# Transfers of the maxima and the spill of the attention rows: issued by ScalarE's queue in place of SP's

## What is computed

```python
qkv = jnp.einsum('bnc,ce->bne', x, w_qkv)          # 16 heads of 8 channels
attn = jnp.einsum('bhnd,bhmd->bhnm', q, k) / scale
attn = jax.nn.softmax(attn, axis=-1)
out = jnp.einsum('bhnm,bhmd->bhnd', attn, v)       # then w_out
...
x = x + _layernorm(_L0_attn_ref(_layernorm(x, axis=-1), ...), axis=-1)
x = x + _layernorm(_L0_ffn_ref(_layernorm(x, axis=-1), ...), axis=-1)
```

## Time and profile before

| | us |
|---|---|
| median of 3 runs | 390.42 (388.07 to 392.32) |
| the profiled execution | 389.27 |
| its span | 387.4 |
| TensorE busy in it | 369.4 (95%) |
| VectorE, ScalarE, GpSimd busy | 305.3, 263.3, 201.9 |

### The profile page before, as it was taken

One profiled execution on the slowest core, in us unless ns is written; L12 is line 12 of the kernel. 1 busy time (PEld: TensorE's weight loads), 2 busy tenths in 40 slices (PEclk: granted clock), 3 DMA queues, 4 the chain that ended last, 5 costly groups with the idle time before them and its releaser, 6 DMA issues.

```text
span 387.4 us, 10179 instructions
## 1 busy us (share of the span) xinstructions
PE 369.4 (95%) x3376; PEld 239.9 (62%) x3376; DVE 305.3 (79%) x775; ACT 263.3 (68%) x498; POOL 201.9 (52%) x521
## 2 busy tenths in 40 slices
PE   7989999998999999999999999999999999998982
PEld 6976655555555757475656565665665656577872
DVE  4238968879999998989998989989999875667540
ACT  2413387787887787868788868787868788753422
POOL 4321041244538384747476646656545648577654
PEclk9998999999999999999999999999999999999997
DMA  1794756385556557554474373747374033223230
GB/s 44 194 208 92 206 131 143 95 200 124 165 120 165 148 138 165 146 136 140 128 181 122 111 185 72 188 128 167 105 185 120 12 105 92 70 62 80 54 85 27
DMA packets 63651, 48.81 MB, mean 126 GB/s; under 512 B 9432, under 2 KB 60504, under 8 KB 63600
## 3 DMA queue, kind: packets, MB, share of 16 engines
q1 hardware_dynamic: 63600, 48.17, 49.0%
HBM read 28.52 MB, written 19.14 MB: 123 GB/s over the span
## 4 chain that ended last, share of the span: by engine, by line
PE 74%; issue 6%; DVE 6%; POOL 5%; SPq 3%; ACT 2%; DMA 2%; POOLq 0%; ACTq 0%; DVEq 0%
PE pvp L475 14%; PE bank_d L573 10%; PE sc L459 9%; PE sc L444 8%; PE bank_d L586 7%; PE bank_d L574 7%; PE bank_d L482 5%; PE bank_a L527 4%; DVE mx L736 3%; PE bank_a L536 2%; PE bank_d L564 2%; POOL rstd L852 2%; PE bank_d L546 2%; DMA den<-pv_dram 1%; PE bank_a L517 1%
## 5 line engine op out<-in xcount | busy, mean ns | idle before, releaser
L736 DVE TENSOR_REDUCE mx<-sc 128x4 f32<-128x1024 f32 x128 | 153.3, 1219 | 23.0 <-PE sc L444 22.3
L608 ACT ACTIVATE pr<-sc 128x1024 f32<-128x1024 f32 x128 | 130.5, 1024 | 19.8 <-PE sc L459 18.9
L475 PE MATMUL pvp<-pr,va 128*32 128x256 f32 x1024 | 68.5, 385 | 0.0
L573 PE MATMUL bank_d<-x3T,wg_sb 128*128 128x256 f32 x160 | 54.7, 424 | 2.4 <-DVE hb L815 2.2
L444 PE MATMUL sc<-ks,qs 48*128 48x256 bf16 x512 | 49.1, 275 | 2.7 <-DVE mx L736 1.7
L459 PE MATMUL sc<-qs,ks 51*128 51x256 bf16 x512 | 49.2, 273 | 0.9 <-ACT pr L608 0.5
L910 POOL TENSOR_TENSOR hw<-hb,rwb 128x256 f32<-128x256 f32 x64 | 45.5, 727 | 4.7 <-DMA rwb<-rw_dram 4.7
L574 PE MATMUL bank_d<-x3T,wu_sb 128*128 128x256 f32 x160 | 47.6, 379 | 0.0
L675 ACT ACTIVATE th<-bank_d 128x256 f32<-128x256 f32 x80 | 30.6, 382 | 21.5 <-PE bank_d L574 20.3
L852 POOL TENSOR_TENSOR rstd<-vareps,mhalf 128x2 f32<-128x2 f32 x64 | 44.5, 695 | 0.0
L482 PE MATMUL bank_d<-ident 128*128 128x128 f32 x264 | 41.2, 301 | 1.5 <-POOL ident L835 1.5
(11 more groups left out here) (80 smaller groups left out, 520.2 us busy)
## 6 DMA issues: line engine op xcount, KB each, us to landing
rwb<-rw_dram SPq DMA_DIRECT2D x32, 256.0 KB, 4.4
qk_dram<-parts SPq DMA_DIRECT2D x32, 192.0 KB, 2.7
qs<-qk_dram SPq DMA_DIRECT2D x32, 192.0 KB, 4.4
ks<-qk_dram SPq DMA_DIRECT2D x32, 192.0 KB, 4.4
qk_dram<-parts SPq DMA_DIRECT2D x32, 128.0 KB, 2.4
pv_dram<-pv_sb SPq DMA_DIRECT2D x16, 256.0 KB, 2.6
x_sb<-in_L_attn_x_dram SPq DMA_DIRECT2D x16, 128.0 KB, 2.6
qk_dram<-parts SPq DMA_DIRECT2D x32, 64.0 KB, 2.0
```

Source lines behind the costliest of these rows:

```text
L475: mm = pe.matmul(pvp[32 * j:32 * j + 32, g, :], values[:, X * c + 4 * g + j, 32 * tt:32 * tt + 32], pr[:, k, c * N:(c + 1) * N], start=(tt ...
L573: pe.matmul(bank_d[bank][:, 0:N], wg_sb[:, ORDER[n], :], x3T[b % 2][:], start=True, stop=True)
L608: nc.scalar.activation(pr[:, 2 * s:2 * s + 2, :].rearrange("p k n -> p (k n)"), sc[PAIR["s2", b, s]][:].rearrange("p u c n -> p (u c n)"), ...
L736: nc.vector.tensor_reduce(mx[b % 2][:, :, :, s].rearrange("p c u -> p u c"), sc[PAIR["s1", b, s]][:], AX.X, ALU.max).then_inc(max_done, 1)
```

## The change

Both blocks of SP's program move to ScalarE's, each right behind the copy whose result it sends. The waits go along: ScalarE now waits for its own copy's semaphore (`max_copied`, `pv_copied`), and ahead of the spill for the loads of two images before. The ticks of max_stack and pv_spill stay in the tables and move nothing any more. The transfers, their shapes, and what waits for them are as before.

```diff
--- before.py
+++ after.py
@@ -378,17 +378,6 @@
                                      qk_dram[b % 2][0, :, :, u].rearrange("a d x n -> (a d) (x n)")).then_inc(qk_stacked[b % 2], DMA)
                         sp.dma_start(ks[b % RING][rows].rearrange("p x n -> p (x n)"),
                                      qk_dram[b % 2][1, :, :, u].rearrange("a d x n -> (a d) (x n)")).then_inc(qk_stacked[b % 2], DMA)
-                if (b := due(tick, "max_stack")) is not None:
-                    sp.wait_ge(max_copied, b + 1)
-                    for u in range(2):
-                        sp.dma_start(qs[b % RING][64 * u + ROWS:64 * u + ROWS_MAX].rearrange("p x n -> p (x n)"),
-                                     mT[b % 2][3 * X * u:3 * X * u + 3 * X, :]).then_inc(max_stacked[b % 2], DMA)
-                if (b := due(tick, "pv_spill")) is not None:
-                    sp.wait_ge(pv_copied, b + 1)
-                    if b >= 2:
-                        sp.wait_ge(oc_loaded[b % 2], landed(1, b - 2))
-                        sp.wait_ge(den_loaded[b % 2], landed(1, b - 2))
-                    sp.dma_start(pv_dram[b % 2].rearrange("g p n -> p g n"), pv_sb[b % 2][:]).then_inc(pv_spilled[b % 2], DMA)
                 if (b := due(tick, "den_load")) is not None:
                     sp.wait_ge(pv_spilled[b % 2], landed(1, b))
                     if b >= 2:
@@ -613,6 +602,10 @@
                     if b >= 2:
                         act.wait_ge(max_stacked[b % 2], landed(2, b - 2))
                     nc.scalar.copy(mT[b % 2][:], bank_a[0:3 * H, 0:N]).then_inc(max_copied, 1)
+                    act.wait_ge(max_copied, b + 1)
+                    for u in range(2):
+                        act.dma_start(qs[b % RING][64 * u + ROWS:64 * u + ROWS_MAX].rearrange("p x n -> p (x n)"),
+                                      mT[b % 2][3 * X * u:3 * X * u + 3 * X, :]).then_inc(max_stacked[b % 2], DMA)
                 if (b := due(tick, "apply1")) is not None:
                     act.wait_ge(x_load[b % 4], DMA * (b // 4 + 1))
                     if b >= 2:
@@ -644,6 +637,11 @@
                     if b >= 2:
                         act.wait_ge(pv_spilled[b % 2], landed(1, b - 2))
                     nc.scalar.copy(pv_sb[b % 2][:], pvp[:]).then_inc(pv_copied, 1)
+                    act.wait_ge(pv_copied, b + 1)
+                    if b >= 2:
+                        act.wait_ge(oc_loaded[b % 2], landed(1, b - 2))
+                        act.wait_ge(den_loaded[b % 2], landed(1, b - 2))
+                    act.dma_start(pv_dram[b % 2].rearrange("g p n -> p g n"), pv_sb[b % 2][:]).then_inc(pv_spilled[b % 2], DMA)
                 if (b := due(tick, "proj_copy")) is not None:
                     act.wait_ge(proj_done, b + 1)
                     if b >= 2:
```

## The result

| | before | changed |
|---|---|---|
| median, us (runs on one chip) | 389.25 (4) | 408.6 (4) |
| ratio of the times, 95% interval | | 1.0518, 1.0465 to 1.0571 |
| profiled execution, its span | 389.27, 387.4 | 406.42, 404.5 |
| TensorE, VectorE, ScalarE busy | 369.4, 305.3, 263.3 | 370.0, 306.1, 262.4 |

What follows compares the result with a forecast made beforehand. The prediction took TensorE to bound the kernel. Its terms, 13.0 + 1.6 - 1.0 - 3.5 = +10.1 us on 389.27, gave 399.4, with the median of three runs 1.15 above the profiled execution: forecast 400 us, range 388 to 410.

Steps and rivals of the forecast that it cites:

- case D: ScalarE becomes the bound, if image 12 is the rule and the spill is never hidden: +20, 410 us; chance 0.09.
- The price of an issue: ScalarE stands 1.72 us behind each copy of maxima and 0.51 behind each spill, by SP's own issue durations.
- rival B: ScalarE's queue issues without holding the engine's arithmetic, so only the 1.0 us gain is left: 388 us; chance 0.08.
- The walks: Delay reaching TensorE from issues behind the maxima's copy, traced in images 8, 12, 5: mean 0.8 us, times 16, +13.0 us.
- Rival A: The hold is hidden anyway, images like 5 being the rule at 0.2 us each: +3, 392 us; chance 0.18.
- Given back by VectorE, -3.5: Where ScalarE makes TensorE late, VectorE gains time, so TensorE's 7.5 us of waits for maxima shrink by half: -3.5 us.
- The spill, +1.6: ScalarE's hold behind the spill's copy falls mostly where work waits anyway: 0.1 us an image, +1.6 us.
- Gain of 1.0 us: TensorE's three waits for the maxima's transfer go, since issues now follow the copy at once: -1.0 us.
- Rival C: SP is the hidden brake, freeing it gives about 384 us, if the hold costs TensorE under 0.36 us an image; chance 0.07.

Runs made afterwards that it cites:

- the run with spare issues: Against the kernel before: all real transfers stay on SP, ScalarE also issues two unneeded transfers behind each copy of maxima; 400.65 against 388.39 us.
- the run with the spare transfer: Against the kernel before: all real transfers stay on SP, ScalarE issues one unneeded 32 KB transfer behind each copy of attention rows; 391.18 against 388.25 us.
- one by one: Against the kernel before: only the maxima's transfers on ScalarE, first behind the operation following the copy, second behind the one after; 397.41 against 388.25 us.

## Why the prediction was right, and where its sum was off

The direction and the range held; of the 20 us the sum found 10. The measured 408.6 us lies above the forecast's own band of 394 to 407, in the part of the range that was kept for case D, 1.4 us under the range's end. That the range held is partly luck.

- **The price of an issue.** Predicted 1.72 us behind the maxima and 0.51 behind the spill, each with the 0.10 us of lost overlap; the gaps are 1.65 and 0.50, so 1.75 and 0.60 with it. Right within 0.1 us, with SP's durations as the source. Whether an issue is small beside its transfer the rows of before couldn't say, since none times the maxima's landing. The rival B, an issue that doesn't hold the engine, was wrong here and right elsewhere: it needs an operation already handed over, as behind an exp.
- **The walks.** Predicted 1.0, 1.45 and 0 us for images 8, 12 and 5; the waits were 0.91 and 1.49, and the distances to the next image in the run with spare issues grew by 1.1, 1.6 and 0.0. The mean of the three walks, 0.8, was also that of all fifteen distances; with distances from 0.0 to 1.6 us, three images could as well have missed it. Rival A needed images like 5 to be the rule, and only two of the fifteen distances are 0.2 us or less. +13.0 was predicted, +13.0 measured by the hold alone, with an interval of 9.9 to 16.2.
- **Given back by VectorE, -3.5.** The largest error: nothing was given back. VectorE works behind ScalarE too. The tanh stands behind the same hold, and VectorE's products wait for it, 16.4 us against 9.2 before, in front of the next maximum. TensorE's waits for maxima rose from 7.5 to 9.4. I had let one wait shrink where the engine behind it was late for the same reason. In image 8 VectorE waits 0.62 us for the tanh, and the maximum of the scores written by 191.47 + 0.39 = 191.86 starts 0.77 us later:

```profile
191.84 0.42 DVE L807 SCALAR_TENSOR_TENSOR ha<-th,bank_d 128x256 f32<-128x256 f32 x1 [0.62 <-ACT th L673]
192.29 0.42 DVE L813 SCALAR_TENSOR_TENSOR hb<-ha,bank_d 128x256 f32<-128x256 f32 x1
192.63 1.22 DVE L734 TENSOR_REDUCE mx<-sc 128x4 f32<-128x1024 f32 x1
```

- **The spill, +1.6.** Measured 4.6, of which 3.4 is the hold. One walked image where it is hidden was too little: the exps' waits show 10.3 us in 27 places in the run with the spare transfer, against 8.4 in 24. Image 10, the one walked, has other work there; with the spill on ScalarE, an exp is the next operation behind the copy in four of the sixteen images, after gaps of 0.49 to 0.57 us. Here the term was mis-sized, not wrong in kind.
- **Gain of 1.0 us.** The term was too large from the start. It added the waits of the weight loads, 0.7 us, and of the matmuls, 0.3, and these are the same pause: at 227.85 both kinds of row end theirs, 0.57 and 0.33 us. The places are two and not three, and at most 0.7 us could be gained. Nor did it come: the waits went from 0.7 to 1.9 us at the weight loads and from 0.3 to 1.4 at the matmuls. The issue is at once behind the copy, but SP's big transfers are no longer behind it.
- **Rival C** fell by its own condition: the hold costs 0.8 us an image, more than 0.36. Nor was there anything to weigh against it: SP's shed issues brought transfers forward that nobody waits for, and in images 6 and 7 these met the one somebody waits for; GpSimd's wait for the routing weights stayed, 4.6 us after 4.7.
- **Rival D** has the nearest number, 410 us, but ScalarE did not become the bound: it is busy for 65% of the span, and with its queue it holds 16% of the chain.

Take the two parts as measured alone, 14.0 for the maxima with all that goes with them and 4.6 for the spill: the sum is 18.6 us, against 20.2; the interval of the whole alone is 2 us to either side. Over the forecast's 10.1 the 18.6 are 3.5 us that VectorE didn't give back, 3.0 of the spill, the 1.0 us of gain that did not come, and 1.0 between the real and the spare transfers of the maxima, which is within the intervals.

## What to carry to other kernels

A transfer issued right behind the result it sends costs the computing engine its whole issue, 0.37 to 0.73 us each here, since nothing is left for it to run; put behind one long operation that is already handed over, more than half of it ran beside (0.9 of 1.52 us). What a hold costs depends on the slack: one issue cost 2.5 us in all, two 13 to 14. Before moving issues off a queue that only issues, look for waits that end on those transfers (here at most 0.7 us), and for what that queue's order keeps apart. A term of relief for another engine is only worth writing down if that engine doesn't itself wait on the one that is slowed.

## What the runs showed of the hardware that I had not expected

- An issue on ScalarE and an operation of ScalarE start in the same moment (189.66, 0.60 us of standing for 1.52 of issue).
- A small transfer on a queue of its own was not sooner: 5.9 us from the end of its issue to the end of the wait, beside four transfers of 192 KB issued within 0.5 us of its first issue (image 6 one by one, image 7 right behind the copy), and at most 4.0 and 4.3 us where they followed it on the same queue.
- Stalls of TensorE can cost more than their length: with holds of 3.1 us the granted clock was down to 0.57 over 20 us, and the same matmuls took 397.0 us in place of 369.4, on top of 36.7 us more without work.
